# Feed-forward weights of a decoder kernel split into halves during the first attention and read back from DRAM

## What is computed

```python
x = x + attn(layernorm(x))            # causal self attention, 16 heads of 64
x = x + xattn(layernorm(x), ctx)      # linear cross attention, 16 heads of 16
x = x + ffn(layernorm(x))             # two layers (DEPTH = 2), here called feed-forward part
# one ffn layer:
h = shift_token(x); q, k, v = split(h @ wqkv)           # wqkv: 256 x 1536
q, k = rotary_xpos(l2norm(q) * qs, l2norm(k) * ksc)     # 8 heads of 64
x = x + local_attention(q, k, v) @ wo                   # windows of 128, look one window back
h = layernorm(shift_token(x)) * lg + lb
a, g = split(h @ w1 + b1)                               # w1: 256 x 1364
x = x + (a * gelu(g)) @ w2 + b2
```

## Time and profile before

| | us |
|---|---|
| median of 3 runs (1185.81 to 1186.63) | 1186.11 |
| the profiled execution | 1185.69 |
| its span, first to last instruction | 1183.9 |
| TensorE busy | 1148.3 |
| VectorE / ScalarE / GpSimd busy | 817.5 / 692.3 / 567.4 |

### The profile page before, as it was taken

One profiled execution on the slowest core, in us unless ns is written; L12 is line 12 of the kernel. 1 busy time (PEld: TensorE's weight loads), 2 busy tenths in 40 slices (PEclk: granted clock), 3 DMA queues, 4 the chain that ended last, 5 costly groups with the idle time before them and its releaser, 6 DMA issues.

```text
span 1183.9 us, 19712 instructions
## 1 busy us (share of the span) xinstructions
PE 1148.3 (97%) x6678; PEld 893.5 (75%) x6678; DVE 817.5 (69%) x2443; ACT 692.3 (58%) x1696; POOL 567.4 (48%) x618
## 2 busy tenths in 40 slices
...
DMA packets 30275, 46.15 MB, mean 39 GB/s; under 512 B 4577, under 2 KB 18017, under 8 KB 30177
## 3 DMA queue, kind: packets, MB, share of 16 engines
...
...
## 4 chain that ended last, share of the span: by engine, by line
PE 87%; DVE 5%; ACT 3%; POOL 3%; issue 2%; DMA 0%; DVEq 0%; ACTq 0%; POOLq 0%
PE psum L1486 53%; PE psum L1587 6%; PE psum L1569 6%; PE psum L1719 5%; PE psum L1768 5%; PE psum L1753 5%; PE psum L1735 4%; PE psum L1701 2%; ACT hnT_hi L958 1%; DVE stats L1030 1%; POOL rn L730 1%; ACT hnT L958 1%; PE psum L1781 1%; DVE xn L1039 0%; PE psum L1675 0%
## 5 line engine op out<-in xcount | busy, mean ns | idle before, releaser
L691 POOL TENSOR_TENSOR probs<-probs,rden 128x128 f32<-128x128 f32 (+3 forms) x256 | 176.5, 721 | 194.6 <-DVE rden L1097 194.6
L928 ACT ACTIVATE lp<-lp,lneg,rn 128x256 f32<-128x256 f32 (+1 forms) x256 | 143.8, 571 | 20.3 <-DVE lneg L1326 20.1
L840 ACT ACTIVATE probs<-probs,negmax 128x128 f32<-128x128 f32 (+3 forms) x256 | 140.7, 551 | 15.8 <-DVE negmax L1092 15.1
L1085 DVE CUSTOM_DVE_ANT_0 probs<-psum,causal 128x512 f32<-128x512 f32 (+3 forms) x256 | 109.9, 485 | 12.7 <-PE psum L1486 12.7
L730 POOL TENSOR_TENSOR rn<-ssm,neg_half 128x8 f32<-128x8 f32 x64 | 106.1, 1658 | 0.0
L1314 DVE CUSTOM_DVE_ANT_0 lp<-psum,local 128x256 f32<-128x256 f32 (+1 forms) x256 | 84.1, 385 | 22.7 <-PE psum L1719 22.6
L721 POOL TENSOR_TENSOR lp<-lp,lrden 128x768 f32<-128x768 f32 x64 | 94.9, 1483 | 0.0
L1486 PE MATMUL psum<-w,hid 124*128 124x256 f32 (+2 forms) x384 | 85.7, 379 | 2.6 <-DVE hid L1390 2.6
L1569 PE MATMUL psum<-ident,probs 128*128 128x128 f32 x640 | 86.0, 273 | 1.5 <-DVE pT L1106 1.1
L1486 PE MATMUL psum<-q,k_rest 128*128 128x256 f32 (+2 forms) x256 | 85.5, 345 | 1.6 <-DVE rowmax L1085 1.6
L1486 PE MATMUL psum<-wqkv_hi,hT_lo 128*128 128x512 f32 x192 | 82.8, 431 | 1.0 <-ACT lv L805 0.9
...
## 6 DMA issues: line engine op xcount, KB each, us to landing
k<-k_round SPq DMA_DIRECT2D x128, 128.0 KB, 2.4
x<-in_x SPq DMA_DIRECT2D x8, 512.0 KB, 6.1
...
ctxT<-in_ctxT SPq DMA_DIRECT2D x4, 512.0 KB, 8.5
x_scratch<-x SPq DMA_DIRECT2D x4, 512.0 KB, 3.2
x<-x_scratch SPq DMA_DIRECT2D x4, 512.0 KB, 6.4
wqkv_raw<-in_wqkv SPq DMA_DIRECT2D x1, 1536.0 KB, 11.7
```

The costliest lines, as they stand in the source:

```text
L691: ins = pool.tensor_tensor(pr, pr, rden[:, u % 2, h, i:i + 1].broadcast_to([P, TRI[i]]), ALU.mult)
L840: ins = act.activation(pr, pr, ACT.Exp, bias=negmax[:, u % 2, h, i:i + 1], scale=ADH ** -0.5, accum_out=den[:, u % 2, h, i:i + 1])
L928: ins = act.activation(pr, pr, ACT.Exp, bias=lneg[:, u % 2, h, w:w + 1], scale=rn[:, m % 2, w, 0, 2 * j + h:2 * j + h + 1], accum_out=lden ...
L1085: ins = dve.tensor_tensor_reduce(probs[:, u % 2, h, TRI_AT[i]:TRI_AT[i + 1]], bank[:, at:at + TRI[i]], causal[:, S - TRI[i]:S], 1.0, -3e38 ...
```

## The change

**What it does.** On the host `wqkv`, `w1`, `w2` and `wo` of both layers are laid out by partitions in one tensor `w_all` of 8360 columns per layer, cut into 11 pieces of 760. In units 4 to 25 of the first attention one piece each (22 for two layers) is loaded by SP, rounded by ScalarE (item part, ahead of t1), subtracted in place by GpSimd (part, behind f of both heads) and stored as two halves into the DRAM tensor `w_dram`. SP's load of piece u-5 and its two stores of piece u-6 follow the key copies of unit u. The buffers lie where y is written later. The tables are made in unit 28 and after norm2.1, stored in `tab_dram`, and loaded into one buffer `tab` per layer. The later splits on ScalarE and VectorE (weights, w1_parts, tab) disappear; finished halves are loaded instead: for layer 0 the rests of qkv behind the last pv and the rounded halves when awo.3's matmuls have ended, for layer 1 when the last q, k and v tiles of layer 0 have. In the entry q.0.0 stands ahead of xo.2 and xw.1 on TensorE. START, ENTRY and CLOSE are written anew for all engines. The spare matmuls are 24 ahead of xT.0 and 18 behind it; pv.0 stands ahead of pk.0 and pq.0.

```diff
+W_SIZE = (E2 * INNER,) * 3 + (E2 * 2 * HID, NF * D, FPAIRS * D)
+W_AT = [sum(W_SIZE[:i]) for i in range(len(W_SIZE) + 1)]
+W_PARTS = 11
+FIRST_PART = 4
+W_PART = W_AT[-1] // W_PARTS
-RUN_IN = 24
-RUN_MID = 14
-RUN_MORE = 16
+RUN_FIRST = 24
+RUN_SECOND = 18
...
         k_rest = sbt(raw, "k_rest", [P, 2, S], F32R)
+        w_raw = sbt(raw, "w_raw", [P, 2, W_PART])
+        w_half = sbt(raw, "w_half", [P, 2, W_PART], F32R)
...
-        START_PE = ("xT.0 pq.0 pk.0 pv.0 xT.1 s.0.0 s.0.1 pk.1 xT.2 pq.1 pv.1 t.0.0 pv.2 s.1.0 t.0.1 "
+        START_PE = ("xT.0 pv.0 xT.1 pk.0 pq.0 pv.1 s.0.0 s.0.1 pk.1 pq.1 pv.2 t.0.0 t.0.1 xT.2 s.1.0 "
...
-        START_DVE = ("xs.0 xn.0 xT.0 aw.0.0 aw.0.1 xs.1 aw.0.2 xn.1 pk.0 pq.0 xs.2 xs.3 xT.1 s.0.0 xn.2 "
+        START_DVE = ("xs.0 xn.0 xT.0 xs.1 aw.0.0 aw.0.1 aw.0.2 xn.1 xs.2 pk.0 pq.0 xT.1 xs.3 s.0.0 xn.2 "
...
-        UNIT_ACT = ("t1 e0@1 pk@2 t3 t5 aw0 pq@2 aw1 e1@1 pv@2 aw2")
-        UNIT_POOL = ("f0@6 f1@6")
+        UNIT_ACT = ("part t1 e0@1 pk@2 t3 t5 aw0 pq@2 aw1 e1@1 pv@2 aw2")
+        UNIT_POOL = ("f0@6 f1@6 part@6")
...
-                    "KV.1 xo.0 xq.1 x1T.2 kv.3 xw.0 awo.3 xq.2 KV.2 KV.3 xo.1 x1T.3 hT.0 xo.2 xq.3 xw.1 "
-                    "q.0.0 k.0.0 q.0.1 k.0.1 xw.2 q.0.2 k.0.2 Tqk.0.0 v.0.0 v.0.1 Tqk.0.1 v.0.2 q.0.3 "
+                    "xq.1 KV.1 xo.0 x1T.2 kv.3 xw.0 awo.3 xq.2 KV.2 xo.1 x1T.3 KV.3 hT.0 xq.3 q.0.0 xo.2 "
+                    "k.0.0 q.0.1 xw.1 k.0.1 Tqk.0.0 v.0.0 v.0.1 q.0.2 k.0.2 q.0.3 Tqk.0.1 k.0.3 v.0.2 "
...
-                    "q3@1 Tqk2@1 fb2 k3@1 tab@5 fa3 hid4@-1 Ta2 hid5@-1 weights@2 hT@2")
+                    "Tqk2@1 fb2 k3@1 fa3 hid4@-1 Ta2 hid5@-1 hT@2")
...
+            def load_part(i):
+                l, c = divmod(i, W_PARTS)
+                sp.dma_start(w_raw[:, i % 2, :], a["w_all"][l, :, c * W_PART:(c + 1) * W_PART])\
+                    .then_inc(ld_part[i % 2], 16)
+
+            def store_part(i):
+                l, c = divmod(i, W_PARTS)
+                sp.wait_ge(part_lo, i + 1)
+                for half, tile in enumerate((w_half, w_rest)):
+                    sp.dma_start(w_dram[l, half, :, c * W_PART:(c + 1) * W_PART], tile[:, i % 2, :].bitcast(F32))\
+                        .then_inc(part_st, 16)
...
             quad_weights(1)
+            load_part(0)
+            load_part(1)
...
             for u in range(NU):
                 other_half(u)
                 c, j, b, pair = unit_at(u)
+                i = u - FIRST_PART - 3
+                if 0 <= i < DEPTH * W_PARTS - 2:
+                    sp.wait_ge(part_st, 2 * 16 * (i + 1))
+                    load_part(i + 2)
+                if 0 <= i + 1 < DEPTH * W_PARTS:
+                    store_part(i + 1)
...
-            sp.dma_start(wqkv_raw[:, :, :], a["wqkv"][0].rearrange("(k p) c -> p k c", p=P)).then_inc(ld_wqkv, 16)
+            for c in range(3):
+                layer_wqkv_lo(0, c)
...
+            sp.wait_ge(l_tab, 6 * DEPTH)
+            for l, done in enumerate((tab_first, rot)):
+                sp.dma_start(tab_dram[l], done[:, :, :, :].rearrange("p a t d -> p (a t d)")).then_inc(tab_st, 16)
+            sp.wait_ge(tab_st, 16 * DEPTH)
+            wait_full(sp, plan["awo", B - 1, 1])
+            for c in range(3):
+                layer_wqkv_hi(0, c)
+            wait_read(sp, plan["kv", B - 1, T - 1])
+            layer_tab(0)
...
+            wait_full(sp, plan["q", B - 1, T - 1])
+            layer_wqkv_lo(1, 0)
+            layer_wqkv_hi(1, 0)
+            wait_full(sp, plan["k", B - 1, T - 1])
+            layer_wqkv_lo(1, 1)
+            layer_wqkv_hi(1, 1)
+            wait_read(sp, plan["q", B - 1, T - 1])
+            wait_read(sp, plan["k", B - 1, T - 1])
+            layer_tab(1)
+            wait_full(sp, plan["v", B - 1, T - 1])
+            layer_wqkv_lo(1, 2)
+            layer_wqkv_hi(1, 2)
...
+            def rest_of_part(i):
+
+                pool.wait_ge(part_hi, i + 1)
+                pool.tensor_tensor(w_rest[:, i % 2, :], w_raw[:, i % 2, :], w_half[:, i % 2, :], ALU.subtract)\
+                    .then_inc(part_lo, 1)
...
+            def round_part(i):
+
+                act.wait_ge(ld_part[i % 2], 16 * (i // 2 + 1))
+                if i >= 2:
+                    act.wait_ge(part_st, 2 * 16 * (i - 1))
+                copy(w_half[:, i % 2, :], w_raw[:, i % 2, :]).then_inc(part_hi, 1)
...
                     if m % B == 0:
-                        pe.wait_ge(w_lo, 3 * l + "qkv".index(what) + 1)
+                        pe.wait_ge(ld_wqkv["qkv".index(what)], 2 * 16 * (l + 1))
```

More of the change, by code:

```diff
@@ L84, in constants, with build @@
             "c_rot": np.ascontiguousarray(rot)}
-def build(nc, a, out, x2_dram):
+def build(nc, a, out, x2_dram, w_dram, tab_dram):
     with ExitStack() as ctx:
@@ L213, in build @@
         raw.close()
-        wqkv_hi = sbt(ctx, "wqkv_hi", [P, E2, 3 * INNER], F32R)
+        wqkv_hi = sbt(ctx, "wqkv_hi", [P, 3, E2, INNER], F32R)
         sq = sbt(ctx, "sq", [P, 2, INNER])
-        tab = [sbt(ctx, f"tab{l}", [P, 4, T, FDH]) for l in range(DEPTH)]
-        rot = tab[DEPTH - 1]
-        qk_scale = sbt(ctx, "qk_scale", [P, DEPTH, 2, FDH])
+        tab = sbt(ctx, "tab", [P, 4, T, FDH])
         hT_hi = sbt(ctx, "hT_hi", [P, E2, S + 1], F32R)
@@ L427, in unit_items @@
                     items.append((what, n, i))
+                if what == "part" and 0 <= n - FIRST_PART < DEPTH * W_PARTS:
+                    items.append((what, n - FIRST_PART))
                 if what == "aw" and j == QUNITS - 3 and c < QUADS - 1:
@@ L777, in _ @@
                     probabilities(*at)
+                if what == "part":
+                    rest_of_part(*at)
                 if what == "norm2":
@@ L782, in _ @@
                     query_norms(*at)
-                if what == "weights" and at[0] == 0:
+                if what == "zeros":
                     set_zeros()
@@ L941, in evac_O @@
                 copy(loT[:, FPAIRS - 1 - u % FPAIRS, :], bank[:, :]).then_inc(read[use[0]], 1)
-            def split_w1(l):
-                act.wait_ge(ld_w1, 16 * (l + 1))
-                for e in range(E2):
-                    copy(w1_hi[:, e, :], w1_raw[:, e, :]).then_inc(w1_hi_ok, 1)
             def evac_hnT(m):
@@ L999, in _ @@
                     evac_xo(*at)
-                if what == "weights":
-                    round_weights(*at)
-                if what == "w1_parts":
-                    split_w1(*at)
+                if what == "part":
+                    round_part(*at)
                 if what == "hT":
@@ L1520, in project_qk @@
                 pe.wait_ge(a_lo, 3 * c + (i + 1))
+                use = plan[("pk", "pq")[i], u]
+                bank = wait_free(pe, use)
                 cols = slice(j % 2 * P, (j % 2 + 1) * P)
@@ L1685, in qkv_tile @@
                     if m % B == 0:
-                        pe.wait_ge(w_lo, 3 * l + "qkv".index(what) + 1)
+                        pe.wait_ge(ld_wqkv["qkv".index(what)], 2 * 16 * (l + 1))
                 use = plan[what, m, t]
                 bank = wait_free(pe, use)
-                cols = slice("qkv".index(what) * INNER, ("qkv".index(what) + 1) * INNER)
+                c = "qkv".index(what)
                 rows = slice(t * P, (t + 1) * P)
-                product(bank[:, :], [(h[:, e, rows], w[:, e, cols]) for e in range(E2)
+                product(bank[:, :], [(h[:, e, rows], w[:, c, e, :]) for e in range(E2)
                                      for h, w in ((hT_lo, wqkv_hi), (hT_hi, wqkv_lo), (hT_hi, wqkv_hi))])\
```

189 lines of the change are left out of this document (85 added, 104 removed), and 83 rows, old and new, of tables (CLOSE_DVE, ENTRY_ACT, ENTRY_DVE, ENTRY_PE).

## The result

The changed kernel took 1197.88 us (median of 4 runs, 1195.34 to 1198.63) against 1186.24 us (4 runs) of the kernel before on the same chip: ratio 1.0093, 95% interval 1.0077 to 1.0109. The forecast was 1179.4 us, faster, with a range up to 1187.5: wrong in sign and outside the range. The profiled execution has a span of 1196.6 us, 12.7 more than the 1183.9 of before. A few executions further down, the profiled one of e9 among them, ran far slower than all others of their kernel; the ratios leave them out.

The account below looks back on a forecast made before the run. It took TensorE, busy 97% of the span, as the bound, with 10.9 us of its idle time in the entry. Terms -5.0 - 1.7 - 1.0 + 1.0 = -6.7 us from 1186.11 gave 1179.4 us, range 1173.0 to 1187.5.

Parts of the forecast that it names:

- VectorE against GpSimd: First attention: GpSimd's subtraction can hold VectorE's negmax; 0.05 us per unit, +1.0 us, bounds 0 and 6.6.
- rival 2: First attention: negmax held behind each GpSimd subtraction, or pieces late ahead of t1; kernel slower, 1189.4 us; chance 0.12.
- The line of 0.35 us a unit: First attention: loss per unit that decides for rival 2, the gain of 7.7 us over 22 units.
- The tables: Unit 28 and after norm2.1: 1.7 us of VectorE each where TensorE bounds; 0, at most +1.
- The entry: Entry into the feed-forward part: new order and relieved VectorE halve TensorE's 10.9 us idle; -5.0 us, bounds -1 and -10.9.
- the clock: Entry, 541 to 547: the clock drop behind the 2.21 us gap goes; -1.7 us, bounds 0 and -1.7.
- the second layer: Near 754: TensorE's wait behind VectorE's weight rests and rest of hT goes; -1.0 us, bounds 0 and -1.24.
- the loads of the finished halves: Ahead of the first query tile and in layer two: loads land in time; 0, if late up to 4 us.
- the start: Up to the first scores: fewer spare matmuls, pv.0 first; 0, bounds -1.5 and +2.5.
- The close: Closing orders at the kernel's end: same work in nearly the same order; 0, bounds -1.5 and +1.
- SP and the DMA queue: First attention: one load and two stores per unit land in time; cost 0, 0.4 us to spare plus 0.7.

Follow-up runs that it names:

- e9: e4 with the loads of pieces 0 and 1 issued behind the key copies of units 1 and 2; 1182.93 us, ratio to the kernel before 0.9959.
- e7: The changed kernel with the piece's subtraction replaced by a one-operand multiplication by a constant, same 760 columns, still behind f1; 1186.26 us (one run).
- e8: The changed kernel with the piece's subtraction cut into four instructions of 190 columns, still behind f1; 1185.92 us, ratio to the kernel before 0.9987.
- e1: The changed kernel with GpSimd's subtraction, from piece 5 on, moved between f0 and f1; 1185.22 us, ratio to the kernel before 0.9986.
- e3: The changed kernel with the first table moved on VectorE from unit 28 to just ahead of the second; 1194.42 us, ratio to the kernel before 1.006.
- e4: The changed kernel with the changes of e1 and e3 together; 1183.30 us, ratio to the kernel before 0.9968.
- e6: e4 with xo.2 and xw.1 put back ahead of the first query tile; 1193.24 us, ratio to the kernel before 1.0047.
- e12: e4 measured once more, beside a repeat of e9 on one chip; 1183.15 us, ratio to the kernel before 0.9962.
- e2: The changed kernel with GpSimd subtracting only 8 of a piece's 760 columns and the second store writing the raw piece; 1183.6 us (one run).

## Why the prediction was wrong

**The step that failed: "VectorE against GpSimd".** It took +1.0 us, with 6.6 as the upper bound; the first attention paid 13.5 (units 9 to 25) and some 0.4 behind them. The mechanism was seen, and it was rival 2; the size of the term, its bound and the 0.12 were the error.

(a) The cover was the larger error. The step took a hold of up to 0.98 us and counted VectorE's holes of 0.7 to 0.9 us, the key's slack and the transposes' 0.5 as cover, so that 0.3 a unit was left at most and 0.05 was taken. They are one chain, negmax, exponentials, pT, TensorE. Measured, 13.5 of some 18 us held in units 9 to 25 came through: only about 0.3 us a unit were covered, not 0.7. Single small holds fare better: e7 has most units at 11.46 us with 0.52 over, and e8 lost 0.75 of 5.8 us; so the chain's slack is about half a microsecond (an estimate from these), and it is gone when longer holds follow each other.

(b) The size of a hold. 0.98 is what would be left of the subtraction (to 215.7) when negmax starts at 214.72; no row shows it, though the prediction calls it one. The idea was right, since negmax does wait for the rest of GpSimd's instruction. The number was low as a bound: up to 1.63 us over 0.17 were measured, 1.14 on average.

(c) GpSimd's price, a part of (b). 1.47 us came from an in-place multiplication by a broadcast operand; subtracting two tensors of 760 columns takes 1.82 us undisturbed (1.89 on average).

The line of 0.35 us a unit, from which the change was to lose, was passed by far: measured was 0.79. Rival 2 had half of 0.98 not hidden and named 1189.4; about three quarters of 1.14 came through.

**The hole was chosen by its length.** The prediction placed the piece into 3.66 us in which GpSimd is idle. Between f0 and f1 the hole is shorter (2.63 us in most units of before, as little as 1.63 in some), and there e1 pays nothing in units 9 to 25, since VectorE then works mostly on PSUM. The rows for that were in the timeline of before: negmax at 214.72 starts 0.47 us behind f1's end.

The trace of before had shown the hold already: the pair of table rows at 1.56 us beside a 1.32 us rotation, and the six negmax rows above. The Trainium skill, SBUF — State Buffer, section "SBUF: two separate sides", calls the port pair that VectorE and GpSimd share an exclusive lock, where the VectorE instruction runs in a two-port mode, or has two SBUF inputs while GpSimd's reads SBUF: whoever starts first keeps it for the whole instruction and the other is fully blocked. Negmax has one SBUF input, and no row shows its mode. If the rule covers it, each negmax behind a subtraction waits for its end, and the trace agrees to 0.03 us (146.58 against 146.56). In e7 the measurement differs from the rule: there negmax ended 1.27 us before GpSimd's instruction. The prediction had weighed a milder sentence of another page.

**The tables: "0, at most +1".** The second stayed free. The first, in unit 28, cost 3.2 us (e3), or about 2 in an undisturbed attention (e4 against e1): priced with GpSimd idle, it runs beside GpSimd's multiplications, and in a unit where TensorE bounds there is no room for 3.6 us.

**The entry: -5.0 and the clock: -1.7.** Measured together -3.2. The gap of 2.21 us fell to 0.48 and the clock stayed at 1.00 behind it, as forecast; e6 bears out that the order is needed for it. But the other waits did not halve. The timeline of the changed kernel, and the stretch around them:

```profile
552.37 0.63 PE L1726 MATMUL psum<-ident,ra 128*128 128x128 f32 x4 [0.48 <-POOL ra L796]
...
612.52 1.06 PE L1726 MATMUL psum<-ident,ra 128*128 128x128 f32 x8 [1.44 <-DVE lpT L1367]
...
620.62 1.13 PE L1744 MATMUL psum<-lkT,lqT 64*128 64x256 f32 x8 [1.38 <-DVE lmax L1345]
```

```profile
612.13:622.08 9.95, 7.74 (x45) 5.93 (x47) 5.17 (x17) 6.97 (x21) 3.56 (x5) 0.83 1.01 398
```

The waits for VectorE's lpT and lmax were there before (1.96 and 1.38 us, near 594 and 607) and stay; of 9.8 us idle 7.6 are left, where the forecast had 5. Around them the granted clock is 0.83 for 9.95 us, a loss of 1.7. That drop comes and goes with the execution: e1, whose entry runs the same orders, shows 1.00 there and takes 213.6 us from unit 31 to the first hnT against 215.2, but has 0.94 over its last 37.6 us. From the mark of unit 31 to the end both take the same, 759.9 us in the changed kernel and 760.0 in e1, against 764.4 before. Behind that mark the trace of before has two such drops (near 541 and 1105), the changed kernel and e1 have one each, e12 has two and e2 none. So single traces don't tell whether the clock's -1.7 was gained; with one drop in the entry on either side the waits brought 3.2.

**Right:** the second layer (forecast -1.0: TensorE's idle time from the first to the last hnT but two falls by 1.2 us, and the wait near 754 is gone), the loads of the finished halves (no wait of TensorE names them) and the start (0; -0.7 up to unit 8).

**The close: 0** looks right (the last step and the end came out 0.3 us longer together), but by luck. The newly written order has two waits that before lacks. The timeline of TensorE in the changed kernel:

```profile
1151.42 1.10 PE L1806 MATMUL psum<-y,shift 128*128 128x512 f32 x2 [0.83 <-issue]
...
1159.22 0.98 PE L1817 MATMUL psum<-ident,hn 128*128 128x128 f32 x7 [0.86 <-DVE hn L1403]
```

In this step TensorE is idle for 2.61 us of 44.84, where before had 0.95 of 44.45. The profiled execution of before had a clock drop in it (0.96), and the changed kernel's had none; e12, which has the drop too, takes 46.47. At the same clock the new closing order is some 2 us slower.

**SP and the DMA queue: 0**, with 0.4 and 0.7 us to spare, was nearly right: transfers landed in 3.9 to 4.7 us instead of 3.5 and ScalarE waited 7.9 us for them. In e1, with the same transfers, it is 2.1 us, and the unit takes 11.53.

With the two misplaced things put right (e4, e12) the change brings about 4 us (ratios 0.9968 and 0.9962) where the forecast had 6.7. By e4's marks, entry and clock brought 3.3 of 6.7 us and units 28 to 31 cost 1.1; against that the start brought 0.6 and units 9 to 25 cost nothing.

## What to carry to other kernels

Where GpSimd gets work, look not for the longest hole of GpSimd but for the stretch in which VectorE reads PSUM; an instruction of VectorE on the critical chain such as negmax (TENSOR_SCALAR, from SBUF to SBUF) is held until GpSimd's two-operand instruction ends, however small it is. Look in the trace of before for its rows that are longer than the median: they show which instructions are held. If the place can't be chosen, cut GpSimd's instruction so that one hold is shorter than the chain's slack (here about half a microsecond). And compare parts of two traces only with the granted clock of both at hand. Holes on several engines are not added up where they lie on one chain: take the chain's own slack.

## What had not been expected

- A VectorE instruction of 0.17 us took up to 1.80 us beside a GpSimd subtraction and ended with it; a VectorE operation with PSUM as one input stayed at 0.68.
- A one-operand GpSimd instruction of 2.11 us held it only until 0.84 us after its own start.
- A reciprocal of the same size as negmax was not held by the subtraction.
- When VectorE's rest of a quad weight had started first (207.44, 0.68 us), it was GpSimd's subtraction (207.46) that took longer, 2.35 us instead of 1.82.
- Four subtractions of 190 columns cost GpSimd 2.26 us against 1.83 for one of 760, and made the kernel 12 us faster.
- Moving two pieces of cross-attention back ahead of the first query tile cost 9.9 us, about half of it by the clock.
